# The reciprocal root of the output norm: one POOL power, or twelve steps on VectorE

## What is computed

```
y = _gated_delta_rule(q, k, v, g.transpose(0, 2, 1), beta.transpose(0, 2, 1))
y = y.transpose(0, 2, 1, 3)
yn = y * lax.rsqrt(jnp.mean(y * y, -1, keepdims=True) + EPS)
yn = norm_weight * yn * jax.nn.silu(z)
return yn.reshape(Bx, Tx, VAL_DIM) @ W_out.T
...
x = x + _L0_attn_ref(_layernorm(x, axis=-1), ...)
x = x + _L0_ffn_ref(_layernorm(x, axis=-1), ...)
```

## Time and profile before

| | |
|---|---|
| Median of the timed runs | 1118.99 us (1117.88 to 1121.29) |
| The profiled execution | 1115.1 us, its span 1113.4 us |
| PE busy | 969.2 us (87%) |
| DVE busy | 672.8 us (60%) |
| POOL busy | 620.2 us (56%) |
| ACT busy | 491.2 us (44%) |
| Mean granted TensorE clock | 0.859 of full speed |

### The profile page before, as it was taken

How to read it: one execution, slowest core, us unless ns; L and a number is a source line. 1 busy time by engine, 2 the same in 40 slices (tenths; PEclk the granted TensorE clock), 3 DMA queues, 4 the chain that set the end, 5 groups by cost and what they waited for, 6 DMA issues and landing times.

```text
span 1113.4 us, 31656 instructions
## 1 busy us (share of the span) xinstructions
PE 969.2 (87%) x12419; PEld 832.0 (75%) x12419; DVE 672.8 (60%) x1626; ACT 491.2 (44%) x938; POOL 620.2 (56%) x775
## 2 busy tenths in 40 slices
PE   3876899998999998899999989997487688999998
PEld 2764688788778788788877877887486355888887
DVE  6368947665766767586576658557824244444446
ACT  4533345453544545454354536343142222555552
POOL 3031238866885886787588568753314111665663
PEclk8687879779887988988797799869678798999999
DMA  6647027339565943946694380011052904444558
GB/s 244 205 101 210 1 50 196 116 101 252 156 177 153 275 135 89 282 119 182 171 255 135 78 229 16 25 50 35 30 209 75 362 29 133 134 148 149 154 183 294
DMA packets 181617, 165.32 MB, mean 148 GB/s; under 512 B 75219, under 2 KB 173916, under 8 KB 180576
## 3 DMA queue, kind: packets, MB, share of 16 engines
q10 hardware_dynamic: 70768, 72.65, 23.1%
q1 hardware_dynamic: 103072, 73.78, 22.4%
q0 software_dynamic: 7632, 16.87, 4.6%
HBM read 65.76 MB, written 101.55 MB: 150 GB/s over the span
## 4 chain that ended last, share of the span: by engine, by line
PE 49%; POOL 18%; DVE 12%; issue 8%; ACT 2%; DMA 2%; SPq 0%; POOLq 0%; DVEq 0%; ACTq 0%
PE ps L1653 7%; POOL arena L810 7%; POOL arena L807 6%; PE ps L1678 4%; PE ps L1563 4%; DVE arena L1146 4%; POOL nrm L773 3%; PE ps L1472 3%; PE ps L1428 3%; PE ps L1482 3%; PE ps L1492 3%; PE ps L1580 3%; PE ps L1644 2%; PE ps L1461 2%; PE ps L1541 2%
## 5 line engine op out<-in xcount | busy, mean ns | idle before, releaser
L1146 DVE SCALAR_TENSOR_TENSOR arena<-ps,cw,arena 128x256 f32<-128x256 f32 x384 | 155.3, 474 | 43.3 <-ACT arena L932 43.3
L1428 PE MATMUL ps<-work,arena 128*128 128x259 f32 x512 | 161.5, 472 | 15.4 <-DVE arena L1146 9.7
L1428 PEld LDWEIGHTS ps<-work,arena 128*128 128x128 f32 x512 | 117.1, 238 | 43.2 <-DVE arena L1146 11.2
L862 POOL DMA_INDIRECT picked<-work x95 | 94.3, 993 | 77.9 <-issue 57.1
L851 POOL DMA_INDIRECT slotted<-hr,slots x64 | 63.5, 993 | 101.7 <-DVE slots L1297 85.6
L810 POOL TENSOR_TENSOR arena<-arena 128x31 f32<-128x31 f32 (+15 forms) x186 | 109.9, 591 | 14.6
L1335 DVE TENSOR_TENSOR work<-work,ps 128x128 f32<-128x128 f32 (+1 forms) x111 | 34.1, 307 | 125.8 <-ACT work L1043 120.1
L807 POOL TENSOR_TENSOR arena<-arena 128x31 f32<-128x31 f32 (+15 forms) x186 | 95.0, 511 | 12.4
L1653 PE MATMUL ps<-arena,work 128*128 x380 | 97.8, 380 | 0.0
L932 ACT ACTIVATE arena<-ps,cw 128x256 f32<-128x256 f32 x128 | 58.0, 472 | 87.7 <-PE ps L1428 72.8
L832 POOL TENSOR_TENSOR work<-work,ec 128x512 f32<-128x512 f32 x32 | 34.0, 1062 | 88.8 <-PE ps L1521 66.2
(11 more groups left out here) (231 smaller groups left out, 2215.4 us busy)
## 6 DMA issues: line engine op xcount, KB each, us to landing
slotted<-blank ACTq DMA_DIRECT2D x17, 4128.0 KB, 18.9
arena<-in_w SPq DMA_DIRECT2D x2, 6528.0 KB, 27.3
arena<-tab SPq DMA_DIRECT2D x96, 128.0 KB, 4.5
work<-slotted SPq DMA_DIRECT2D x95, 129.0 KB, 2.1
arena<-picked SPq DMA_DIRECT2D x8, 1024.0 KB, 14.5
work<-tab SPq DMA_DIRECT2D x32, 128.0 KB, 3.7
arena<-in_w_qkv SPq DMA_DIRECT2D x1, 2048.0 KB, 7.5
xin<-in_x SPq DMA_DIRECT2D x16, 128.0 KB, 5.2
```

What stands on the lines that cost most here:

```text
L862: g.indirect_dma_start(out=picked, out_offset=bass.IndirectOffsetOnAxis(ap=to, axis=0), in_=yrow(j), in_offset=None, bounds_check=TOPK * T ...
L1146: v.scalar_tensor_tensor(out=acc_, in0=bank_of("proj", p, s_, i)[:, k:k + W2], scalar=cw[:, u, k:k + 1], in1=acc_, op0=ALU.mult, op1=ALU.a ...
L1428: ins = mm(to[:, 0:WX], wqkv[:, k, m:m + P], xt2[:, p % 3, k, :], start=k == 0, stop=k == KD - 1)
```

## The change

The stage `npow` leaves the tables and POOL's queue. In the stage `yn`, VectorE waits for `nin` (its own earlier instruction), computes the reciprocal root of the 16 columns with `rsqrt`, and then scales as before. `nrm` grows from two rows to four, for the two temporaries. The unneeded semaphore `npow_out` goes.

```
-    "npow": [(156.4, 0), (186, 1)],
...
-        nrm = sb("nrm", 2, NV)
+        nrm = sb("nrm", 4, NV)
...
-                if name == "npow":
-                    b, = ix
-                    pool.wait_ge(S["nin_out"], b + 1)
-                    power(nrm[:, 1, :], nrm[:, 0, :], "npow_out")
...
                 if name == "yn":
                     b, = ix
-                    dve.wait_ge(S["npow_out"], b + 1)
+                    dve.wait_ge(S["nin_out"], b + 1)
+                    rsqrt(*(nrm[:, k, :] for k in (1, 0, 2, 3)))
                     o = otok[:, b % 2, :, :, :].rearrange("p e h d -> p (e h) d")
```

More of the change, by code:

```diff
@@ L179 @@
     "nin": [(152.8, 0), (177.3, 1)],
-    "npow": [(156.4, 0), (179.4, 1)],
     "yn": [(159.5, 0), (193.1, 1)],
@@ L254 @@
     "nin": [(144.6, 0), (165, 1)],
-    "npow": [(146.7, 0), (167, 1)],
     "yn": [(149.8, 0), (170.2, 1)],
@@ L280 @@
 PER_CHUNK = ("kqs", "ebload", "ktb", "v", "ks", "qs", "r", "sd", "u", "up", "ue", "ku", "su", "au", "oe")
-PER_BLOCK = ("osq", "nin", "npow", "yn", "yt", "yg", "op", "x2", "xin", "lnp", "xn", "rmp", "hh", "base", "hr", "ht", "htb", "rt", "mx", "ex",
+PER_BLOCK = ("osq", "nin", "yn", "yt", "yg", "op", "x2", "xin", "lnp", "xn", "rmp", "hh", "base", "hr", "ht", "htb", "rt", "mx", "ex",
              "tk", "rank", "slot", "send", "blanks")
@@ L585, in gated_delta_moe @@
             "kqs_out", "ks_mm", "qs_mm", "sd_out", "r_out", "u_mm", "ue_out", "up_out", "ku_mm", "s_out", "au_mm", "o_out",
-            "osq_out", "nin_out", "npow_out", "yn_out", "z_mm", "zs_out", "yt_mm", "yg_out", "op_mm", "x_in", "x2_out", "norm_in",
+            "osq_out", "nin_out", "yn_out", "z_mm", "zs_out", "yt_mm", "yg_out", "op_mm", "x_in", "x2_out", "norm_in",
             "norm_pow", "h_out", "hr_out", "base_out", "base_stored", "h_t", "htb_in", "ht_stored", "rt_mm", "rt_in", "rt_exp",
```

## The result

| | before | after |
|---|---|---|
| Median of the timed runs | 1118.43 us (1105.40 to 1121.29, 4 runs) | 1154.56 us (1147.42 to 1163.25, 4 runs) |
| Ratio | 1 | 1.038 (1.033 to 1.043) |
| The profiled execution, span | 1115.1, 1113.4 us | 1163.25, 1161.5 us |
| PE busy, and span less PE busy | 969.2, 144.2 us | 976.0, 185.5 us |

The kernel is slower by 3.8%, about 42 us. 1185 us were forecast; 1154.56 lies in the range of 1136 to 1203, but in the part of rival 1 and its mixtures (1134 to 1165, chance 0.24). The main case, 1165 to 1203, did not come.

A forecast was written before the change was run, and what follows sets the result against it. TensorE, busy 87%, was taken as the bound, without slack at the odd blocks' second yt. Odd 37.8, even 26.1 and last four blocks 2.5 make 66.4 us, on 1119.0 giving 1185 us; range 1136 to 1203.

The forecast's parts named there:

- rival 1: At yn in the first twelve blocks only the root's first step waits for POOL: 1141 us, mixtures to 1165; chance 0.24.
- The main case: Most root steps blocked by POOL's elimination in the first twelve blocks, clock cost included: 1165 to 1203 us, chance 0.64.
- What is removed: Sixteen POOL powers of 2.93 us; six odd blocks' waits of 3.7 us return, POOL's earlier end is worth nothing.
- The mechanism: Root steps at yn wait for POOL's elimination: each 0.20 us up to a POOL step of 0.35 to 0.69 us.
- the row of L1256: Profile row at 384.96: one-operand tensor_scalar, begun 0.03 us ahead of a POOL instruction, took 1.22 us and not 0.4.
- The near tie: Beside the elimination, DVE's next root step (0.03 + 0.03 us) against POOL's next instruction (0.07 us gap): POOL wins.
- six odd blocks, to the second yt: First six pairs: the root beside the elimination delays the second yt by 6.3 us per odd block, 37.8 us in all.
- six even blocks, to the second yt: First six pairs: second yt later by 2.1 us in pair 3, 6.0 in pair 4; 26.1 us in all.
- The top-k work: Odd blocks, ahead of yn: L1277, L1283 and L1285 now meet elimination steps and lose about 0.8 us.
- Rival 4: Longer gaps lengthen TensorE's 1.2 GHz stretches: about 3 us per pair, up to 18, 1203 us; counted within chance 0.64.
- Block 14: Among the last four blocks: a gain of 1.7 us, since DVE waited 3.66 us there for a late power.
- The Trainium skill against the rows: By the page, removing the power frees 2.9 us of port per block; by the rows there is no such gain.

The follow-up runs named there:

- power_kept_beside: The change, with POOL still computing the power at its old place, result unused: 1151.14 us, 1.028 times the kernel before.
- no_root: The change without the root, so neither power nor root, scaling by the unrooted mean squares: 1103.78 us, 0.992 times the kernel before.
- pool_pauses: The change, with POOL waiting for the scaling where its power stood, so the root runs beside idle POOL: 1148.63 us, 1.027 times the kernel before.
- one_sbuf_operand: The change, with the iterate y in a PSUM bank and the products reordered: 1135.12 us, 1.023 times the kernel before.
- root_at_nin: The change, with the same twelve steps computed directly behind nin, not at yn: 1147.19 us, 1.034 times the kernel before.
- power_earlier: The kernel before, with POOL taking the odd blocks' power six elimination instructions earlier: 1109.73 us, 0.996 times the kernel before.
- idle_one_sbuf: The change, with y in PSUM and the odd block's root moved ahead of mx; even roots stay at yn: 1130.50 us, 1.015 times the kernel before.

## Why the prediction was off

**What bounds the kernel: right where it counts.** The prediction saw no slack between DVE's yn and the second yt of the odd blocks. L1567 after waits 4.21 us in the block where L1573 had none of it, and 47.2 us in all, and the odd stretch grows with the root. That TensorE is the bound because it is busy holds less there: the odd stretch took 24.5 us before at mean granted clocks of 0.86 and of 0.93 alike, so it was already DVE's queue that set it.

**What is removed: right where it says nothing is gained from POOL.** POOL waits 4.42 us at the sends, "some 4 us or more" was forecast, and power_kept_beside bears it out. The removal without any root is worth 9 us (no_root; 0.5 to 1.2%), where 5.4 was forecast, and no wait shows where they come from.

**The mechanism: right.** The new steps wait for POOL's elimination (pool_pauses, one_sbuf_operand), the one-operand ones too: L1060 takes 0.51 us and L1062 0.45, and both 0.17 when POOL stands still. Both were taken from the row of L1256.

**The near tie: wrong, and this is the term that was mis-sized.** The main case counted the blocking of most steps. The prediction put DVE's 0.03 + 0.03 us against POOL's gap of 0.07 and gave every round to POOL. DVE gets in each time, for one step, and POOL holds the next. In the six odd roots not one step breaks the alternation. Rival 1 had the first half of that, and expected only the first step to wait; the truth lies midway. That the range holds the time is owed to its covering these mixtures, which had a chance of 0.24. The row of L1256 was not wrong, it was the wrong neighbour: it stood beside `sd`, an independent instruction of POOL, and beside such ones every step does wait (root_at_nin). The elimination's instructions depend on one another, and the step that slips in starts in their gap of 0.07 us.

**The sums.** In the profiled executions, by the delay that each stretch adds. The odd blocks' stretch is the odd stretch from above; the even blocks' one is the last 11 us ahead of their second yt.

| term | forecast, us | measured, us |
|---|---|---|
| six odd blocks, to the second yt | 37.8 | 21.6 (1.4, 4.3, 4.2, 3.7, 4.3, 3.7) |
| six even blocks, to the second yt | 26.1 | 14.9 (2.6, 0.4, 2.9, 2.2, 3.9, 2.9) |
| from the odd block's second yt to its output projection | 0 | 7.4 (0.5, 3.0, 2.8, 1.5, -0.5, 0.1) |
| last four blocks and the rest | 2.5 | 4.2 |
| sum | 66.4 | 48.1 |

In the odd block a root of 4.18 us, 2.1 less than forecast, gives 4.2 in place of 6.3, and five of six blocks measure that within 0.5. In the even blocks the roots were 2.8 to 3.9 us long; in pair 3 the forecast was 5.5 and 3.5 came, in pair 4 7.1 and 3.9.

**The top-k work: too dear.** It was to lose about 0.8 us beside the elimination. In pair 3 L1277 takes 0.38 us instead of 0.29, and L1280 0.46 instead of 0.23; in the other odd blocks up to 0.52 and 0.54. That is 0.3 to 0.5 us.

**The clock: left out of the sum, there in the profile.** Rival 4 had priced it at up to 18 us. After an odd block of pair 1, windows of 3 us in the kernel before and then in the kernel after (the third number from the end is TensorE's granted clock, behind it are DMA share and GB/s):

```profile
312.00:315.00 3.00, 3.00 (x9) 2.37 (x9) 1.17 (x5) 0.47 (x1) 2.53 (x5) 0.56 1.00 336
315.00:318.00 3.00, 3.00 (x15) 2.63 (x14) 2.19 (x6) 1.07 (x2) 2.39 (x3) 1.00 1.08 273
```

```profile
314.70:317.70 3.00, 2.97 (x42) 2.67 (x42) 2.90 (x10) 0.63 (x1) 0.00 (x0) 0.50 0.00 0
317.70:320.70 3.00, 3.00 (x35) 2.71 (x34) 0.95 (x3) 0.00 (x0) 2.03 (x2) 0.50 0.99 331
320.70:323.70 3.00, 3.00 (x8) 2.35 (x7) 0.00 (x0) 0.95 (x2) 2.48 (x4) 0.50 1.09 285
323.70:326.70 3.00, 3.00 (x13) 2.56 (x12) 2.44 (x6) 0.60 (x1) 2.53 (x7) 0.86 1.09 327
```

Before, TensorE is back at the 2.4 GHz level within some 3 us. After the longer wait for yn, with 1.2 us of work from 306 to 312, it works at 0.50, the 1.2 GHz level, until 324.5. This gives most of the 7.4 us between yt and op, in the pairs 1 to 3. It is not a fixed price: in the pairs 4 and 5 nothing is added, and the second profile of the change has waits as long and 19.4 us less busy time.

**Block 14: the gain did not come.** The row of 3.66 us idle time was to be returned. The first step of that root took 1.59 us. It began during a send on POOL, 0.5 us ahead of `sd`, and ended 0.04 us behind `sd`:

```profile
892.34 1.59 DVE L1060 TENSOR_SCALAR nrm<-nrm 128x16 int32<-128x16 int32 x1
```

```profile
892.84 1.05 POOL L829 TENSOR_TENSOR work<-work,ec 128x512 f32<-128x512 f32 x1
```

In power_kept_beside a step of the same block began at 883.60, inside the power's last 0.5 us, and took 1.58 us, to the end of the `sd` behind the power (885.14). So a step that starts ahead of an independent POOL instruction by its record can still wait for it, as L1256 did in the earlier trace rows.

**The Trainium skill against the rows.** The prediction went by the rows where the Trainium skill ("SBUF — State Buffer", Who interferes with whom) has a GpSimd instruction that reads SBUF hold the shared pair for its length. For the elimination, `sd` and `kqs` the runs agree with the Trainium skill, for the power they do not: L1283 has 0.29 us inside it, and 0.54 when power_earlier puts it beside the elimination, and the root's own steps have 0.16 to 0.18 us inside it in power_kept_beside. One operand in PSUM ends the waiting, as the Trainium skill's condition of two SBUF inputs has it. For one-operand steps the Trainium skill, in the same section, names `tensor_scalar` among the operations that can take the shared pair in a 2-port mode; L1060 and L1062 agree, and L1071 in one_sbuf_operand, which writes PSUM, does not tell more, since it is the step that slips in.

## What to carry to other kernels

Ask of an operation that is moved to another engine what runs beside it there, instruction by instruction: twelve steps of 0.17 us cost 2.5 us alone, 4.2 beside dependent POOL instructions, and each one a whole POOL instruction beside independent ones; an operand in PSUM takes 1.1 of the 1.7 us away. An idle stretch of an engine is no free place for work until it is known what the instructions behind it release: moving the root to nin delayed the taps, and pausing POOL delayed the next power in its queue by over 3 us. Where the span varies with the clock, look for a stretch between two fixed instructions that another engine's queue sets. Its length repeats (25.34 or 25.35 us in five pairs at clocks from 0.87 to 0.95), while TensorE's busy and idle time in it trade against each other.

## What the runs showed of the hardware

- Two-operand DVE steps on SBUF alternate beside a chain of dependent POOL instructions (0.40 to 0.51 us and 0.17 to 0.18 us in the odd blocks), and wait one each beside independent ones (0.99, 1.01, 1.01 us).
- A one-operand `tensor_scalar` from SBUF to SBUF waits for POOL as well (0.51 and 0.45 us against 0.17). With one operand of two in PSUM a step does not (0.17 and 0.18 us).
- POOL's power of 2.9 us did not hold up the DVE instructions inside it: L1283 took 0.29 us, the root's steps in power_kept_beside 0.16 to 0.18 us. It so shields those beside it from the elimination. The exception is a step in its last 0.5 us, which waited for the independent `sd` behind it (1.58 us).
- The same program has, with 47.2 and 50.8 us of waits for the scaling, 976.0 and 956.6 us of TensorE's busy time in two executions, at mean granted clocks of 0.854 and 0.872.
- A stretch that DVE's queue sets has the same length at either clock: 25.34 us in idle_one_sbuf with sixteen TensorE matmuls at 0.57 (6.4 us, no wait) and at 1.00 (3.9 us, 2.89 us of wait).
- Left open: how the 9 us of no_root come about, and what pausing POOL gains in time on one and the same chip.
